# Adding the experts' rows onto the output by accumulating scatters, in place of handing the first choices' rows to the second

## What is computed

```python
xf = x.reshape(T, D)                                  # T = 8192
probs = jax.nn.softmax(xf @ gate_w.T, axis=-1)
top_p, top_i = jax.lax.top_k(probs, K)                # K = 2
w = top_p / (jnp.sum(top_p, axis=-1, keepdims=True) + 1e-09)
capacity = int(CAPACITY_FACTOR * T / E)               # 1280
oh = jax.nn.one_hot(top_i, E, dtype=jnp.int32)
my_rank = jnp.sum((jnp.cumsum(oh, axis=0) - 1) * oh, axis=-1)
keep = (my_rank < capacity).astype(w.dtype)
comb = jnp.einsum('tk,tke->te', w * keep, oh.astype(w.dtype))
for e in range(E):
    y = (silu(xf @ gate_proj_w[e].T) * (xf @ up_proj_w[e].T)) @ down_proj_w[e].T
    out = out + comb[:, e:e + 1] * y
...
x = x + ffn(layernorm(x))
```

## Time and profile before

| | us |
|---|---|
| median of 3 runs | 961.66 (960.26 to 963.79) |
| profiled execution, first to last instruction (span) | 951.5 |
| TensorE busy | 827.3 (87%) |
| VectorE busy | 639.4 (67%) |
| GpSimd busy | 541.1 (57%) |
| ScalarE busy | 464.4 (49%) |

### The profile page before, as it was taken

One profiled execution on the slowest core, in us unless ns is written; L12 is line 12 of the kernel. 1 busy time (PEld: TensorE's weight loads), 2 busy tenths in 40 slices (PEclk: granted clock), 3 DMA queues, 4 the chain that ended last, 5 costly groups with the idle time before them and its releaser, 6 DMA issues.

```text
span 951.5 us, 25572 instructions
## 1 busy us (share of the span) xinstructions
PE 827.3 (87%) x9107; PEld 620.1 (65%) x9107; DVE 639.4 (67%) x2064; ACT 464.4 (49%) x772; POOL 541.1 (57%) x747
## 2 busy tenths in 40 slices
PE   3799999999999999888898888884499999789992
PEld 2577777877667777666676666673276666556661
DVE  5888999889667877777777777655155554344551
ACT  1356667667366765666666665651222223122220
POOL 3366656656542266666566665556356666366665
PEclk8899999999999998999999999985699999989997
DMA  7369940000000011111000000111434444346540
GB/s 239 92 229 390 388 169 0 0 1 1 1 2 14 14 58 53 59 45 38 27 30 29 29 29 29 36 44 37 150 108 144 122 148 121 116 136 196 178 151 5
DMA packets 50336, 87.01 MB, mean 91 GB/s; under 512 B 12809, under 2 KB 28105, under 8 KB 50232
## 3 DMA queue, kind: packets, MB, share of 16 engines
q1 hardware_dynamic: 37872, 72.18, 22.6%
q0 software_dynamic: 11264, 12.70, 4.1%
q10 hardware_dynamic: 1096, 0.73, 0.3%
HBM read 42.08 MB, written 58.41 MB: 106 GB/s over the span
## 4 chain that ended last, share of the span: by engine, by line
PE 46%; DVE 12%; issue 9%; another core or an unknown queue 4%; ACT 3%; POOL 2%; DVEq 1%; DMA 1%; POOLq 0%; ACTq 0%
PE psum L1451 8%; PE psum L1927 7%; PE psum L1939 5%; PE psum L1412 4%; PE psum L1462 3%; PE psum L1431 3%; DVE top_score L978 2%; POOL out L1826 2%; PE psum L1417 2%; PE psum L1394 2%; PE psum L1486 1%; PE psum L1398 1%; DVE yo L1864 1%; DVE h L1879 1%
## 5 line engine op out<-in xcount | busy, mean ns | idle before, releaser
L1826 POOL DMA_INDIRECT out<-yo,token x160 | 159.1, 994 | 108.1 <-issue 53.9
L852 POOL DMA_INDIRECT dispatched<-z,idx x128 | 129.8, 1014 | 75.5 <-issue 48.0
L1289 ACT ACTIVATE PT<-psum,key_bias 77x1024 f32<-77x1024 f32 x128 | 136.4, 1105 | 58.3 <-PE psum L1434 56.9
L1431 PE MATMUL psum<-qT,Kb 32*77 32x128 f32 x2048 | 134.9, 284 | 1.8 <-issue 1.6
L1908 ACT ACTIVATE act_g<-psum 128x512 f32<-128x512 f32 x80 | 45.8, 596 | 175.0 <-DVE h L1879 82.5
L978 DVE TENSOR_REDUCE top_score<-psum 128x8 f32<-128x616 f32 x128 | 100.6, 795 | 21.3 <-PE psum L1412 19.7
L1412 PE MATMUL psum<-Kb,qT 32*128 32x308 f32 x512 | 101.9, 468 | 7.0 <-DVE o L987 4.4
L1864 DVE SCALAR_TENSOR_TENSOR yo<-psum,xin,base 128x128 f32<-128x128 f32 x156 | 44.0, 344 | 92.4 <-remote 44.6
L1431 PEld LDWEIGHTS psum<-qT,Kb 32*77 32x77 f32 x2048 | 95.0, 145 | 4.9 <-issue 4.2
L1939 PE MATMUL psum<-down,h 128*128 128x128 f32 x640 | 82.6, 284 | 17.4 <-DVE h L1879 13.4
L1434 PE MATMUL psum<-MT,minus_sel 32*77 32x128 bf16 x1024 | 93.3, 217 | 0.2 <-issue 0.2
...
## 6 DMA issues: line engine op xcount, KB each, us to landing
...
out<-yo,token POOLq DMA_INDIRECT x160
...
```

The source lines that it names most:

```text
L852: pool.indirect_dma_start(xg[k], bass.IndirectOffsetOnAxis(ap=idx[n % Z4][:, t, k:k + 1], axis=0), z4[n % Z4][:, t, :], None, bounds_check ...
L1289: nc.scalar.activation(PT[j % 2][:, half * HB * 2 * P:(half + 1) * HB * 2 * P], T[:, 2 * half:2 * half + 2, :].rearrange("p a c -> p (a c) ...
L1431: nc.tensor.matmul(T[:, q, h * P:(h + 1) * P], Kb[par][rows_of(q), h, j * S2:(j + 1) * S2], qT[g % 3][rows_of(q), j * P:(j + 1) * P], star ...
L1826: pool.indirect_dma_start(rows_out if slot else out, bass.IndirectOffsetOnAxis(ap=token[i][:, t:t + 1], axis=0), yo[i][:, t, :], None, bou ...
```

## The change

`ROW` falls from 261 to 131 floats: the residual, PLACE and ALONE leave the tables, and with them the copy on ScalarE and five operations of 4 columns on VectorE per group of the routing. X is stored to the output as before. Both halves' scatters now add their rows (y x weight, without a residual) onto the output in the transfer (`compute_op=ALU.add`). An empty row adds zeros onto a row of its own behind the tokens' rows (`spare_rows`, which are zeroed as the handed rows were), so no row is out of range. yo is made in one multiplication of 128x512. `load_first`, `base` and the skipped `y_side` at the seam go; GpSimd waits at group 20 until the first half's scatters have landed, and groups 18 and 19 are paced too.

```diff
-X_AT, CODE, PLACE, ALONE, WEIGHT = P, 2 * P, 2 * P + 1, 2 * P + 2, 2 * P + 3
+CODE, WEIGHT = P, P + 1
...
-        zeros = sb("zeros", [P, G4 * ROW])
+        zeros, spare = sb("zeros", [P, G4 * ROW]), sb("spare", [P, G4 * P])
...
-            sp.wait_ge(s["zeros_ready"], 1)
+            sp.wait_ge(s["zeros_ready"], 2)
...
-                             zeros[:, 0:G4 * P]).then_inc(s["zeros_stored"], 16)
+                             spare[:]).then_inc(s["zeros_stored"], 16)
...
+            pool.memset(spare[:], 0.0).then_inc(s["zeros_ready"], 1)
...
-            pool.wait_ge(s["zeros_ready"], 1)
+            pool.wait_ge(s["zeros_ready"], 2)
...
-                pool.wait_ge(s["residual_ready"], g + 1)
                 pool.wait_ge(s["idx_ready"], g + 1)
...
-                    v.tensor_scalar(taken[:], rank[:, :, 1], float(CAP), None, ALU.is_lt)
-                    v.tensor_scalar(z4[g % Z4][:, :, ALONE], rank[:, :, 1], float(CAP), None, ALU.is_ge)
-                    v.scalar_tensor_tensor(away[:], row[:, :, 1], float(ROWS + TOKENS) - NO_TOKEN,
-                                           codes[:, bass.ts(g, G4)], ALU.add, ALU.subtract)
                     ins = v.scalar_tensor_tensor(pair[:], total[:], 1e-9, ex[:, :, E], ALU.mult, ALU.add)
                 if k == 14:
-                    v.tensor_tensor(away[:], away[:], taken[:], ALU.mult)
                     ins = v.tensor_scalar(pair[:], pair[:], 1.0, None, ALU.add)
                 if k == 15:
-                    v.tensor_tensor(z4[g % Z4][:, :, PLACE], away[:], codes[:, bass.ts(g, G4)], ALU.add)
                     ins = v.reciprocal(z4[g % Z4][:, :, WEIGHT], pair[:])
                 if k == 16:
                     ins = v.tensor_tensor(z4[g % Z4][:, :, WEIGHT + 1], z4[g % Z4][:, :, WEIGHT], ex[:, :, E], ALU.mult)
...
-            def residual_side(g):
-                nc.scalar.activation(z4[g % Z4][:, :, X_AT:X_AT + P], X[:, bass.ts(g, G4), :], ACT.Copy).then_inc(s["residual_ready"], 1)
...
                     if j == 0:
-                        if group(g - 2):
-                            residual_side(g - 2)
...
-                residual_side(NG - 2)
                 num_out(NB - 1)
                 gate_exps(NG - 2)
                 for t in range(G4):
                     ln4_apply(NG - 1, t)
-                residual_side(NG - 1)
...
-        rows_out, handed = out[0:TOKENS, :], out[TOKENS:TOKENS + E * CAP, :]
+        spare_rows = sb("spare_rows", [P, K2 * E * CAP // P])
+
+        rows_out = out[0:TOKENS, :]
...
-            def load_first(n, i, p):
-                for k in range(PAIR):
-                    sp.wait_ge(s[f"y{k}_scattered"], 16 * G4 * PAIRS // K2)
-                sp.wait_ge(s["y_ready"], n - PAIR + 1)
-                sp.dma_start(first[i][:], rows_of(handed, n - NE // K2, i)).then_inc(s[f"first{i}_loaded"], 16)
...
-                    if n == SECOND + 1:
-                        load_first(SECOND, 0, p)
-                    if n > SECOND:
-                        load_first(n, i, p)
...
+            sp.dma_start(spare_rows[:], d["spare_rows"]).then_inc(s["spare_loaded"], 16)
...
-                    paced = m < NE - 1 and n not in (SECOND - 2, SECOND - 1)
+                    paced = m < NE - 1
+                    if n == SECOND:
+                        for k in range(PAIR):
+                            pool.wait_ge(s[f"y{k}_scattered"], 16 * G4 * PAIRS // K2)
...
                             pool.wait_ge(s["up_ps"], HC * m + 1)
                         if last:
                             pool.wait_ge(s["tile_ready"], t + 1)
-                        pool.indirect_dma_start(rows_out if slot else out, bass.IndirectOffsetOnAxis(ap=token[i][:, t:t + 1], axis=0), yo[i][:, t, :], None,
-                                                bounds_check=TOKENS - 1 if slot else TOKENS + E * CAP - 1, oob_is_err=False).then_inc(s[f"y{i}_scattered"], 16)
+                        pool.indirect_dma_start(out, bass.IndirectOffsetOnAxis(ap=token[i][:, t:t + 1], axis=0), yo[i][:, t, :], None,
+                                                bounds_check=TOKENS + E * CAP - 1, oob_is_err=True, compute_op=ALU.add).then_inc(s[f"y{i}_scattered"], 16)
...
-                slot = n // SECOND
...
-                v.tensor_scalar(token[i][:].unsqueeze(2), xin[i][:, :, (PLACE, CODE)[slot]:(PLACE, CODE)[slot] + 1], NO_TOKEN, None,
-                                ALU.add).then_inc(s["token_ready"], 1)
-
-            def residual(n):
-                p, i = divmod(n, PAIR)
-                slot = n // SECOND
-                if some(n):
-                    dve.wait_ge(s["y_ready"], n)
-                rows = xin[i][:, :, X_AT:X_AT + P]
-                if slot == 0:
-                    ins = v.tensor_tensor(base[:], rows, over(xin[i][:, :, ALONE], 2, P), ALU.mult)
-                else:
-                    dve.wait_ge(s[f"first{i}_loaded"], 16 * (p - PAIRS // 2) + 16)
-                    ins = v.tensor_tensor(base[:], rows, first[i][:], ALU.add)
-                ins.then_inc(s["base_ready"], 1)
+                v.scalar_tensor_tensor(token[i][:].unsqueeze(2), xin[i][:, :, CODE:CODE + 1], NO_TOKEN,
+                                       spare_rows[:, bass.ts(n, G4)].unsqueeze(2), ALU.add, ALU.min).then_inc(s["token_ready"], 1)
 
             def y_side(n):
                 i = n % PAIR
                 slot = n // SECOND
-                residual(n)
-                dve.wait_ge(s["base_ready"], n + 1)
                 dve.wait_ge(s["y_ps"], n + 1)
-                for t in range(G4):
-                    last = v.scalar_tensor_tensor(yo[i][:, t, :], y_ps[n % 3][:, t, :], xin[i][:, t, WEIGHT + slot:WEIGHT + slot + 1],
-                                                  base[:, t, :], ALU.mult, ALU.add)
-                last.then_inc(s["y_ready"], 1)
+                v.tensor_tensor(yo[i][:], y_ps[n % 3], over(xin[i][:, :, WEIGHT + slot], 2, P), ALU.mult).then_inc(s["y_ready"], 1)
...
-                    if has(n - 1) and n not in (SECOND + 1, SECOND + 2):
+                    if has(n - 1):
                         y_side(n - 1)
...
-                    if n == SECOND + 2:
-                        y_side(SECOND)
-                        y_side(SECOND + 1)
-
+
+            dve.wait_ge(s["spare_loaded"], 16)
             places(0)
             pairs(dve, body)
             i = PAIR - 1
-            residual(NE - 1)
-            dve.wait_ge(s["base_ready"], NE)
             for t in range(G4):
                 dve.wait_ge(s["tile_ps"], t + 1)
-                v.scalar_tensor_tensor(yo[i][:, t, :], banks[t][:, 0:P], xin[i][:, t, WEIGHT + 1:WEIGHT + 2],
-                                       base[:, t, :], ALU.mult, ALU.add).then_inc(s["tile_ready"], 1)
+                v.tensor_scalar(yo[i][:, t, :], banks[t][:, 0:P], xin[i][:, t, WEIGHT + 1:WEIGHT + 2], None, ALU.mult).then_inc(s["tile_ready"], 1)
...
+    def spare_rows():
+        order = []
+        for n in range(K2 * E * CAP // GROUP_ROWS):
+            at = TOKENS + n * GROUP_ROWS % (E * CAP) + np.arange(GROUP_ROWS)
+            order.append(at.reshape(G4, P).T if n % PAIR == PAIR // 2 else at.reshape(P, G4))
+        return c(np.concatenate(order, 1).astype(np.float32))
```

10 lines of the change are left out of this document (4 added, 6 removed).

## The result

The change makes the kernel slower: 997.68 us (994.55 to 1001.65, 4 runs) against 960.96 us (958.29 to 963.79, 4 runs) of the kernel before, ratio 1.0392 with a 95% interval of 1.036 to 1.0424. The forecast was 945.4 us. It is rival A: GpSimd became the bound.

What follows compares the result with a forecast made beforehand. TensorE was taken to bound the expert stage, with a hole at the seam of the halves. 951.5 - 12.3 - 3 - 1.5 + 0.5 = 935.2 us, plus 10.1 around the span, gave 945.4 us; range 939 to 998, likeliest 940 to 954.

Steps and rivals of the forecast that it cites:

- rival A: Expert stage: dearer accumulating scatters make GpSimd the bound from 1.42 us between scatters; time 947 to over 998, chance 40%.
- GpSimd's price: Expert stage's 160 scatters: an accumulating one costs GpSimd 0.973 us like a plain one, 1.28 us apart; counted at nothing.
- Rival A's formula: Expert stage: last scatter ends at 692 + 160 c + 3, 5 us follow; c is the distance between scatters.
- c over 1.8: Costliest part of GpSimd becoming the bound: expert-stage scatters over 1.8 us apart, time over 998 us; chance 10%.
- the dear end: Upper bound for the accumulating scatter on GpSimd: twice the work per row, 2.25 us apart, time 1070 us.
- The seam: Between the expert stage's halves, blocks 20 to 25: waits for handed rows go, -12.3 us, bounds -13.9 and -5.
- The bound of -5: Least gain where the expert halves meet, if late semaphores and not handed rows are most of the hole.
- VectorE's part: Expert groups: 0.44 us less between project_down's end and h, in some 12 groups; -3 us, bounds -5 and 0.
- Ahead of the stage: Before the experts: shorter rows load sooner (1.1) and routing loses five small VectorE operations (0.4); -1.5 us, bounds -3 and 0.
- The tail: After the last scatter: landing with an addition costs +0.5 us, bounds 0 and +3.
- Transfers: Output rows take 32 to 64 us per DMA engine, smaller loads save 47; DMA share stays about where it is, cost nothing.
- 10.1 us around the span: Whole kernel: the run median exceeds the profiled span by 10.1 us, taken as lying around the span and unchanged.

Runs made afterwards that it cites:

- plain_scatter: The changed kernel with the add taken off its 160 output scatters, additions onto the output left out; 944.96 us against 959.6 for the kernel before, ratio 0.9835.
- seam_add3: The kernel before with only groups 20 to 22 accumulating and first handed rows loaded for group 23; 958.0 us against 959.6, ratio 0.9984.
- plain_slow_b: The changed kernel without the add, GpSimd filling an unread 128x512 tile ahead of each scatter; 943.5 us against 899.56 for the kernel before, ratio 1.0499.

## Why the prediction was wrong, point by point

**GpSimd's price (the step that failed).** The sum took the lower bound, 0.973 us, "since both kinds of scatter in the trace cost the same whatever they carry ... which looks like a price per instruction". That reading was right (0.44 of 0.54 us are fixed), the conclusion was not: a price per instruction is one for this kind of instruction, and no row showed the accumulating kind. The forecast hung on a margin of 0.14 us per scatter, and the unknown reached up to 0.97 us: it could hold only if the price stayed at the very lower end. Measured: 1.548 us, 1.85 apart, which is 0.43 us over the 1.42 at which GpSimd becomes the bound. Rival A's formula, 692 + 160 x 1.85 + 8 = 996, is the span seen (999.7) but for a stage that began some 3 us later. By A's own numbers the case was c over 1.8, to which I gave 10%. That 997.7 us still lies inside the wide 939 to 998 is luck: with the 10.1 us that I put around the span, A's formula gives 1006.

The Trainium skill's two sections for the dear end ("Collectives: The Full Stack", "The bandwidth ceiling", and "GPSIMD Engine Reference", "When to use GPSIMD") had the direction, and the 1070 us worked out from them were too much: the instruction takes 1.59 times as long, not twice, and 0.44 of the 0.54 us are there at 16 rows already, which a price per read descriptor doesn't give.

The Trainium skill's "DMA: Bandwidth & Descriptors", section "Anatomy of one DMA", says that many descriptors can be emitted before their cost shows. The rows bear that out (from 16 to 128 rows a plain scatter grows by 0.14 us, an adding one by 0.23); what fails is my step from it to a c near 1.28, since the price is in the instruction and not in the number of rows.

**The seam (right in its place, half right in its cause, and not kept).** In the changed kernel the gain can't be seen, since GpSimd is behind anyway. Without the add on A (plain_scatter) blocks 20 to 25 are 31.4 us apart in place of 42.2: -10.8, where I had -12.3. The cause I gave was half of it: it takes the handed rows and the late signals together, since of 13.85 us on A only 2.9 remain on a chip with signals on time. And the gain isn't kept: the other blocks of the same trace take 7.0 us more than before, with signals late among them (0.6 up to block 20, 6.5 from block 25 on), so that blocks 0 to 39 take 241.5 us in place of 245.3, -3.8; on B it is 219.3 in place of 222.2, -2.9. The bound of -5, "if the late semaphores below, and not the handed rows, are most of it", came nearer to what the stage gave back. seam_add3, with 1.6 us that can't be told from nothing, shows the same. The new wait costs GpSimd 2.4 us, under the 10 allowed; but here GpSimd is the bound, and so they stand in the time.

**VectorE's part: nothing, not -3.** yo went to 0.69 us as foreseen. In plain_scatter blocks 0 to 20 take 120.6 us (120.0 before) and 25 to 39 take 89.6 (83.1). VectorE waited for a late signal and not for its own work, so a shorter yo starts no earlier; the traces show no gain that could be put down to it. On B, without late signals, the groups of the kernel before come every 5.67 us but for the seam and the last two, so there was nothing for a shorter yo to give back. The sentence "Why the signal is late the profile does not say ... I leave that as it is" left open the largest loss of the stage.

**Ahead of the stage: right in size.** From issue to the first transposition 1.85 us less (-1.5 forecast); 2.7 to 3.1 us in every kernel with the short rows, 4.4 to 5.2 in the others, on all chips.

**The tail: not to be seen in the changed kernel,** where GpSimd's backlog makes it 37.7 us. Without the add nothing changed on B: 15.8 us from block 39 to the end in both kernels. The landing with an addition, +0.5, no run isolates.

**Transfers: not the bound, and mis-sized.** The software queue takes 13.0% of 999.7 us, 130 us of each engine, where I had at most 64 for the output and some 13 for the routing's rows. Its 14.78 MB are 9216 packets without the add and 27136 with it. The share of the DMA engines is 0.58 in the first half and 0.49 at the end, against 0.43 and 0.51 before; I had said "about where it is". (The 20.9 MB of rows loaded should read 21.4, which changes nothing.) It still bounds nothing: plain_slow_b has the same pattern of waits at 4.9%.

**10.1 us around the span: wrong.** 1.9 lie around it; the rest was that the profiled execution of before was some 8 us quicker than the median. That plain_scatter, the change without the add, meets the 945.4 us with 944.96 is luck for the most part. Its difference of medians is -14.6 us (-16.3 forecast), but the traces hold only 6.3 us of it (951.5 to 945.2), and of these 3.8 in the stage; the remaining 8 us they don't place, the profiled execution of before being 8 us quicker than its median. On B the same change of code gives -3.8 us. The terms for the seam and VectorE, -15.3 together, stand against 3 to 4 us that the stage gave back on either chip.
